# A layered attention and feed-forward kernel: its loops on every engine written out, with constants for registers

## What is computed

```python
x = L0_attn_x                                        # 4 x 1024 x 128
h = _layernorm(x) * (1 + ca) + sa
x = x + ga * softmax((h Wq + bq)(h Wk + bk)^T / sqrt(128)) (h Wv + bv)
h = _layernorm(x) * (1 + cb) + sb
for i in range(6):                                   # DEPTH
    q, k, v = split(shift_tokens(h) @ Wqkv[i], 3)    # 16 heads of 64
    q, k = rotary(l2norm(q) * qs), rotary(l2norm(k) * ks)
    h = local_attention(q, k, v, window=32) @ Wo[i] + h
    a, gate = split(norm(shift_tokens(h)) @ W1[i] + b1[i], 2)
    h = a * gelu(gate) @ W2[i] + b2[i] + h
x = x + gb * h
```

## Time and profile before

| | |
|---|---|
| median of 3 runs | 3659.52 us (3654.99 to 3666.93) |
| the profiled execution, its own time | 3657.72 us |
| its span, first to last instruction | 3655.9 us |
| mean granted TensorE clock | 0.970 |
| PE busy | 3440.4 us (94%) |
| PEld busy | 2655.9 us (73%) |
| DVE busy | 2639.6 us (72%) |
| ACT busy | 2510.0 us (69%) |
| POOL busy | 2356.1 us (64%) |

### The profile page before, as it was taken

One profiled execution on the slowest core, in us unless ns is written; L12 is line 12 of the kernel. 1 busy time (PEld: TensorE's weight loads), 2 busy tenths in 40 slices (PEclk: granted clock), 3 DMA queues, 4 the chain that ended last, 5 costly groups with the idle time before them and its releaser, 6 DMA issues.

```text
span 3655.9 us, 132252 instructions
## 1 busy us (share of the span) xinstructions
PE 3440.4 (94%) x50548; PEld 2655.9 (73%) x50548; DVE 2639.6 (72%) x5823; ACT 2510.0 (69%) x5117; POOL 2356.1 (64%) x1568
## 2 busy tenths in 40 slices
PE   7979999999999999999999999999999999999997
PEld 5658777777777777777777777777777777777774
DVE  5668777778777778777677777777767677777773
ACT  3447777777666777766677776677767677766773
POOL 2048677677666677666676766677766667666661
PEclk9989999999999999999999999999999999999998
DMA  2001111211111211111111111111111121111111
GB/s 80 2 14 49 34 44 41 62 41 50 36 42 37 62 37 51 40 35 43 58 41 37 50 41 35 50 54 38 52 35 39 36 65 40 47 40 39 41 37 44
DMA packets 98219, 157.34 MB, mean 43 GB/s; under 512 B 18128, under 2 KB 39632, under 8 KB 96720
## 3 DMA queue, kind: packets, MB, share of 16 engines
q1 hardware_dynamic: 93440, 132.73, 13.4%
q10 hardware_dynamic: 4176, 15.74, 1.3%
HBM read 20.48 MB, written 2.10 MB: 6 GB/s over the span
## 4 chain that ended last, share of the span: by engine, by line
PE 78%; issue 7%; ACT 5%; POOL 1%; DVE 1%; ACTq 0%; DMA 0%; DVEq 0%; POOLq 0%; SPq 0%
PE psum L797 20%; PE psum L821 12%; PE psum L887 9%; PE psum L907 7%; PE psum L844 6%; PE psum L864 4%; PE psum L852 4%; PE psum L927 4%; PE psum L939 3%; PE psum L932 3%; PE psum L816 2%; PE psum L918 1%; PE psum L914 1%; ACT probT L592 1%; ACT qbd L585 1%
## 5 line engine op out<-in xcount | busy, mean ns | idle before, releaser
L388 POOL TENSOR_TENSOR qkr<-qks,rnorm 128x1024 f32<-128x1024 f32 x384 | 731.3, 1905 | 388.0 <-issue 291.4
L380 POOL TENSOR_TENSOR qks<-work 128x1024 f32<-128x1024 f32 x384 | 908.0, 2365 | 72.2 <-DVE work L1148 67.9
L396 POOL TENSOR_TENSOR probn<-prob,psumr 128x512 f32<-128x512 f32 x384 | 400.6, 1043 | 542.9 <-DVE psumr L1174 542.9
L575 ACT ACTIVATE sq<-psum 128x512 f32<-128x512 f32 x768 | 463.9, 604 | 366.9 <-PE psum L797 366.2
L797 PE MATMUL psum<-whi,xhi 128*128 128x512 f32 x1152 | 571.8, 496 | 113.0 <-issue 79.1
L1122 DVE TENSOR_REDUCE ssq<-sq 128x8 f32<-128x512 f32 x768 | 516.6, 680 | 54.4 <-ACT sq L575 18.6
L1146 DVE TENSOR_TENSOR work<-psum,rot 128x512 f32<-128x512 f32 x768 | 508.3, 662 | 51.1 <-POOL qks L380 41.9
L1180 DVE TENSOR_REDUCE nmax<-psum 128x8 f32<-128x512 f32 x384 | 265.1, 690 | 380.7 <-PE psum L821 379.4
L821 PEld LDWEIGHTS psum<-kT,qbd 128*64 128x64 f32 x12288 | 411.6, 143 | 127.0 <-issue 126.8
L821 PE MATMUL psum<-kT,qbd 128*64 128x64 f32 x12288 | 468.5, 231 | 13.3 <-issue 13.2
L797 PE MATMUL psum<-whi,xlo 128*128 128x512 f32 x1152 | 464.5, 403 | 0.0
(11 more groups left out here) (131 smaller groups left out, 6488.8 us busy)
## 6 DMA issues: line engine op xcount, KB each, us to landing
vsh<-vtok SPq DMA_DIRECT2D x384, 192.0 KB, 2.4
vsh<-vtok SPq DMA_DIRECT2D x384, 64.0 KB, 3.0
xsh<-xs_in SPq DMA_DIRECT2D x192, 64.0 KB, 2.4
ff_x<-x_mid SPq DMA_DIRECT2D x96, 128.0 KB
wqkv<-Wqkv_dram ACTq DMA_DIRECT2D x5, 1536.0 KB, 6.7
wo_next<-Wo_dram ACTq DMA_DIRECT2D x5, 512.0 KB, 8.2
xtok<-x_dram SPq DMA_DIRECT2D x4, 512.0 KB, 11.0
out_dram<-qkr SPq DMA_DIRECT2D x8, 256.0 KB, 2.5
```

The source lines that it names most:

```text
L380: pool.tensor_tensor(qks[:, :, :], rcos, rsin, ALU.add).then_inc(s["add_ready"], 1)
L388: pool.tensor_tensor(qkr[:, j % 2, :, :], qks[:, :, :], rnorm[:, :].unsqueeze(2).to_broadcast([P, 2 * OCT, DH]), ALU.mult).then_inc(s["qkr ...
L396: pool.tensor_tensor(probn[:, :, :], prob[:, j % 2, :, :], psumr[:, j % 2, 1, :].unsqueeze(2).to_broadcast([P, OCT, KEYS]), ALU.mult).then ...
L575: act.activation(sq[:, w * OCT:(w + 1) * OCT, :], bank[w].rearrange("p (h n) -> p h n", n=DH), ACT.Square).then_inc(s[("sqq_ready", "sqk_r ...
```

## The change

Every engine's program is written out in Python over `STEPS + 2 * UNROLL` = 400 steps, with the absolute unit number n in place of a turn and its offset. There is no loop left on any engine, the output loops included, so every wait value, column and table entry is a constant. `Turn`, `sweep` and `wait_apart` are gone; `need` waits for a constant and is left out where that is zero or less; `block_at` and `renewed_at` say in which steps a feed-forward block or a weight renewal has its place. The same operations stand in the same order on each engine, with the same buffers. Five waits are new on PE: `ffn_mean`, `ffn_variance`, `ffn_up` and `ffn_down` also wait for `pts_ready`, and `output` always waits for `x_mid_ready`.

```diff
-        def need(eng, what, base, off, first=False):
-            if first and off <= 0:
-                return
-            eng.wait_ge(s[what], base + off)
-
-        def wait_apart(eng, *waits):
-            for k, (what, value) in enumerate(waits):
-                eng.reg_mov(counts_of[eng.engine][k], value)
-            eng.wait_ge(s["id_ready"], 1)
-            for k, (what, value) in enumerate(waits):
-                eng.wait_ge(s[what] if isinstance(what, str) else what, counts_of[eng.engine][k])
-
-
-
-        def sweep(eng, body):
-            def turn(layer, it, **more):
-                def v(e):
-                    return e if isinstance(e, int) else eng.snap(e)
-                early = isinstance(it, int) and it < 2
-                body(Turn(units=v(layer * UNITS + it * UNROLL), tiles=v(layer * TILES + it * TPI), block=v(layer * BLOCKS + it - 2),
-                          it=it, layer=v(layer), kb=(it - 2) % BLOCKS if isinstance(it, int) else v(it - 2),
-                          ffn_layer=v(layer - 1 if early else layer), **more))
-
-            turn(0, 0, first=True, ffn=False)
-            turn(0, 1, ffn=False)
-            with eng.Fori(2, ITERS - 1) as it:
-                turn(0, it)
-            with eng.Fori(0, DEPTH - 1) as layer:
-                turn(layer, ITERS - 1, renew=True)
-                turn(layer + 1, 0, renew=True)
-                turn(layer + 1, 1, renew=True)
-                with eng.Fori(2, ITERS - 1) as it:
-                    turn(layer + 1, it)
-            turn(DEPTH - 1, ITERS - 1)
-            turn(DEPTH, 0, last=True)
-            turn(DEPTH, 1, last=True, drained=True)
+        def need(eng, what, value):
+            if value > 0:
+                eng.wait_ge(s[what], value)
...
-                    def attend(j, u):
-                        if j is None:
-                            return
-                        tp, oc = j // UPT % 2, j % UPT
-                        wait_apart(pe, (vsh_in[j % 4], units * 8 + (j // 4 + 1) * 32), ("pts_ready", units + (j + 1)),
-                                   *([] if first and j <= 0 else [("aot_ready", units + j)]),
...
-                    def ffn_mean():
-                        pe.wait_ge(s["f_x"], t.block * 32 + 32)
-                        pe.wait_ge(s["f_out"], t.block)
-                        pe.matmul(bank[4], mean_mat[:, :], ff_x[:, :], start=True, stop=True).then_inc(s["f_m"], 1)
-
...
-                sweep(pe, body)
...
+            def attend(n, ffn_in_67):
+                if not is_unit(n):
+                    return
+                tp, oc = n // UPT % 2, n % UPT
+                pe.wait_ge(vsh_in[n % 4], (n // 4 + 1) * 32)
+                need(pe, "pts_ready", n + 1)
+                need(pe, "aot_ready", n)
+                if ffn_in_67 is not None:
+                    pe.wait_ge(s["f_u"], ffn_in_67 * CH + CH)
...
+            def output(n):
+                if not is_unit(n) or n % UPT == 0:
+                    return
+                tp, tile = n // UPT % 2, n // UPT
+                need(pe, "aot_ready", n + 1)
+                need(pe, "vs_ready", min(n + 4, STEPS))
+                need(pe, "x_mid_ready", tile)
...
+            def ffn_mean(b):
+                if b is None:
+                    return
+                pe.wait_ge(s["f_x"], b * 32 + 32)
+                need(pe, "f_out", b)
+                need(pe, "pts_ready", min(b * UNROLL + 2 * UNROLL - 5 + 1, STEPS))
+                pe.matmul(bank[4], mean_mat[:, :], ff_x[:, :], start=True, stop=True).then_inc(s["f_m"], 1)
...
+            for step in range(STEPS + 2 * UNROLL):
+                ffn_up(block_at(step, 4))
+                projection(step, 0)
+                ffn_down(block_at(step, 5))
+                scores(step - 3)
+                turn_q(step - 2)
+                turn_probabilities(step - 5, (block_at(step, 1), "f_xc", lambda b: b + 1), (block_at(step, 3), "f_ln", lambda b: b + 1),
+                                   (block_at(step, 4), "f_u", lambda b: b * CH + 1), (block_at(step, 5), "f_out", lambda b: b + 1))
+                value_projection(step - 3)
+                projection(step, 1)
+                turn_k(step - 2)
+                attend(step - 5, block_at(step, 4))
+                output(step - 6)
+                ffn_mean(block_at(step, 0))
+                ffn_variance(block_at(step, 2))
...
-                    def ffn_out():
-                        dve.wait_ge(s["f_y"], t.block + 1)
-                        dve.scalar_tensor_tensor(out=xs_in[:, bass.ds(t.kb * BLK + t.kb // 2 + HIST, BLK)], in0=bank[4],
-                                                 scalar=b2_col[:, bass.ds(t.ffn_layer, 1)],
-                                                 in1=x_mid[:, bass.ds(t.kb * BLK + t.kb // 2 + 1, BLK)], op0=ALU.add, op1=ALU.add).then_inc(s["f_out"], 1)
...
+            def ffn_out(b):
+                if b is None:
+                    return
+                layer, kb = b // BLOCKS, b % BLOCKS
+                dve.wait_ge(s["f_y"], b + 1)
+                col = kb * BLK + kb // 2 + 1
+                dve.scalar_tensor_tensor(out=xs_in[:, col:col + BLK], in0=bank[4], scalar=b2_col[:, layer:layer + 1],
+                                         in1=x_mid[:, col:col + BLK], op0=ALU.add, op1=ALU.add).then_inc(s["f_out"], 1)
```

More of the change, by code:

```diff
@@ L10 @@
 from contextlib import ExitStack
-from dataclasses import dataclass
 import concourse.bass as bass
@@ L57, with block_at, renewed_at, is_unit @@
 NORM_AT = {bw: n for n, bw in enumerate(NORMS)}
[L60 to L79, removed]
+def block_at(step, place):
+    b = step // UNROLL - 2
+    return b if step % UNROLL == place and 0 <= b < DEPTH * BLOCKS else None
+def renewed_at(step, place):
+    layer = (step - place) // UNITS
+    return layer if (step - place) % UNITS == 0 and 0 < layer < DEPTH else None
+def is_unit(n):
+    return 0 <= n < STEPS
 def build(nc, x, w_attn, b_qk, b_v, Wqkv, Wo, W1, W2, cols, b1_cols, gains, c_t, wmod, rot_tab, out):
@@ L245, in _ @@
             sp.dma_start(w2[:, :, :].rearrange("p k n -> p (k n)"), W2[0]).then_inc(s["w2_in"], 16)
[L247 to L260, removed]
-                sp.dma_start(dst[0:64], src[0:64, bass.ds(col, width)]).then_inc(signal, 16)
-                sp.dma_start(dst[64:P], src[64:P, bass.ds(col - 1, width)]).then_inc(signal, 16)
@@ L303, in _ @@
+            for step in range(STEPS + 2 * UNROLL):
+                x_half(step)
+                ffn_fetched(block_at(step, 0))
+                values_shifted(step - 4)
             out_v = out.rearrange("b (k t p) d -> (b k) p t d", t=4, p=P)
-            with sp.Fori(0, BLOCKS // 2) as i:
+            for i in range(BLOCKS // 2):
                 for h in range(2):
@@ L312, in _ @@
         def _(pool):
-            counts_of[pool.engine] = [pool.alloc_register(f"pool_count{k}") for k in range(2)]
             pool.memset(ident[:, :], 0.0).then_inc(s["id_zero"], 1)
@@ L451, in _ @@
         @block.scalar
         def _(act):
-            counts_of[act.engine] = [act.alloc_register(f"act_count{k}") for k in range(2)]
             act.preload_act_table_set("natural_log_exp_and_others")
@@ L693, in _ @@
         @block.tensor
         def _(pe):
-            counts_of[pe.engine] = [pe.alloc_register(f"pe_count{k}") for k in range(4)]
             pe.wait_ge(s["silu_ready"], 1)
@@ L962, in _, with project @@
-            pe.wait_ge(s["mask_ready"], 10)
-            attention()
-            with pe.Fori(0, BLOCKS // 2) as i:
+            def project(out, n, w):
+                ti, oc = n // UPT % TPI, n % UPT
+                if n % UNITS < UPT:
+                    pe.wait_ge(s["w_lo"], n // UNITS * len(SECTIONS) + ((0, 1), (2, 3), (4, 5))[oc if w < 2 else 2][w if w < 2 else oc] + 1)
+                for k, (xp, wp_) in enumerate(PARTS):
+                    mm = pe.matmul(out, xparts[xp][:, ti, :], wparts[wp_][:, w, oc * 512:(oc + 1) * 512], start=(k == 0), stop=(k == 2))
+                return mm
@@ new lines, in turn_probabilities @@
+            def turn_probabilities(n, *ffn_in_4):
+                if not is_unit(n):
+                    return
+                need(pe, "pn_ready", n + 1)
+                need(pe, "pts_ready", n)
+                for b, what, value in ffn_in_4:
+                    if b is not None:
+                        pe.wait_ge(s[what], value(b))
+                for a in range(PAIRS):
+                    mm = pe.transpose(bank[4][:, a * P:(a + 1) * P], probn[:, 2 * a:2 * a + 2, :].rearrange("p h n -> p (h n)"), ident[:, :])
+                mm.then_inc(s["pt_ready"], 1)
@@ new lines, in ffn_down @@
+            def ffn_down(b):
+                if b is None:
+                    return
+                pe.wait_ge(s["w2_in"], b // BLOCKS * 16 + 16)
+                pe.wait_ge(s["f_u"], b * CH + CH)
+                need(pe, "pts_ready", min((b + 2) * UNROLL, STEPS))
+                for ch in range(CH):
```

(18 more changed lines are left out.)

890 lines of the change are left out of this document (407 added, 483 removed).

## The result

The changed kernel takes 3473.51 us (median of 4 runs, 3472.59 to 3477.69), the kernel before 3662.82 us on the same chip (4 runs). The ratio is 0.9488, with a 95% interval of 0.9468 to 0.9507: 5.1% faster. The profiled execution took 3472.62 us, against 3657.72 us: 185.1 us less.

The account below looks back on a forecast made before the run. PE, busy 94% of the time, was taken as the bound. Jumps (175.4 us) and renewals (1.5 us), 176.9 us in all, off the profiled 3657.7 gave 3480.8, stated as 3480 us, range 3464 to 3502.

Parts of the forecast that it names:

- The jumps: PE's 28 loop turns with a jump back: 175.4 us would go, 6.3 us a jump.
- the same turn without a jump takes 66.0: Basis of the jump term: all 28 jumping turns, 72.3 us each, would take 66.0 us like an already written-out turn.
- Registers: Register work: DVE's ahead of the feed-forward result lies inside the 6.3 us a jump; nothing added, 8.4 us kept for the range.
- New waits: 384 added waits on PE, in feed-forward functions and output, already met earlier: zero in the sum, 19.6 us if none is hidden.
- Renewals: Weight renewals in the written-out turns: 1.5 us gained, as every layer should look like the 203.1 us three.
- the 7.5 us kept for it in the range: Allowance for each of five renewals meeting a half clock again, 1.5 us each.
- Fetching: Fetching the written-out program once in full: zero in the sum, one 1.10 us PE packet needed every 6.9 us.
- The rival of a late stream: PE would wait for its instruction packets in the 28 turns, 296 us, giving 3776 us, slower than before; chance 4%.
- Output and drain: Small output loop at the end loses three jumps and some register columns: nothing counted.
- The sum: Jumps plus renewals, 175.4 + 1.5 = 176.9 us, off the profiled 3657.7 us gives 3480.8 us.
- The next wait moves up: Rival: without jumps PE waits for lagging POOL, DVE or ACT; half of 6.3 us returns, 3568 us; chance 8%.
- The signs: Trace marks of being right: no PE branches, ordinary turns at 66.0 us, clock near 1.00, fewer than 480 PE fetch packets.

Follow-up runs that it names:

- experiment 2: Changed kernel with only PE back on loops and registers, the other four engines written out: 3661.36 us, 0.9993 of the kernel before.
- experiment 3: Kernel before with PE's inner loops written out, its outer loop (4 jumps) and most registers kept, other engines written out: 3508.30 us, 0.9575.
- experiment 5: Changed kernel plus a two-pass loop around one already met wait at the head of each of PE's 50 turns: 3473.09 us, 0.9477.
- experiment 6: Changed kernel plus four-pass loops of met waits, various sizes, behind the work on PE and ACT; only the jumps' times were read, no kernel time given.
- experiment 1: Changed kernel with only PE written out; SP, POOL, ACT and DVE keep the loops and registers of the kernel before: 3499.97 us, 0.955.
- experiment 9: Changed kernel without the 192 new waits for pts_ready in PE's four feed-forward functions: 3474.06 us, 0.9484.
- experiment 10: Changed kernel with ACT's exponential moved behind the attention copy in the steps with an up projection: 3463.47 us, 0.9455.
- experiment 4: PE with its outer loop alone, other engines written out, and ACT issuing the next layer's weights two steps later: 3494.15 us, 0.9536.

## Why the prediction was right

- **The jumps, 175.4 us.** Right, 176.7 measured. The step "the same turn without a jump takes 66.0" held to 0.05 us a turn, or 1.3 us in all. Experiments 2 and 3 show that PE's jumps carry some 170 us of it, and 5 and 6 that distance decides. The other 6.4 us are step 5 with DVE's registers, as the prediction says when it puts them inside the 6.3 us a jump. Its 6.3 us was a mean over unlike jumps (2.9 and 6.9), which the sum didn't need to know.
- **What the prediction did not see** is that the other engines' outer jumps are worth 24 us once PE's are gone (experiment 1). It read the earlier trace rows as if ACT's 45 ns meant that ACT jumps free. For the inner loop that is true. For the outer one the record is as short, and the stall lies behind it. The number came out right because the change takes away both; for a change of PE alone it would have been 26.5 us too low. The sum took these stalls in, since it compares with turns in which no engine jumps; the mechanism told with it left them out. The rows of before held the hint: of the ten waits for `xlo` in the earlier trace rows, 27.9 us, I gave five to the renewals at the group's mean of 2.8 us. Read one by one, the renewals' five take 2.1 each, one of 2.8 stands ahead of the turns, and the other four, 14.5 us, 3.2 to 3.9 each, stand at the outer jumps, where POOL and ACT came late themselves.
- **Registers: zero beyond the turn of the earlier trace rows.** Right. In experiment 3 PE's cost nothing, in 1 DVE's cost 0.1 us a turn at most. Both together, in before, cost 0.23 us in each loop turn, which the comparison with the turn of the earlier trace rows already took in.
- **New waits: zero, bound 19.6 us.** Right, by experiment 9 for half of them. For the 192 in `output` no run takes them out; the 65.95 us, below the 66.0 of the turn without them, speak for zero.
- **Renewals: 1.5 us.** 3.1 measured: the first trio gave 1.8, the others 0.3 each. The half clock at a renewal comes and goes: in experiment 10 three of five renewal turns take 70.4 to 70.5 us and two 68.9. So some of the 7.5 us kept for it in the range can occur.
- **Fetching: zero.** Right. 404 packets over the span, 65.95 us in every ordinary turn, and no idle time of PE over 0.4 us in one. The threes of before had fetched 25 packets each and not the 29 of the rival's text, and after needs one every 8.0 us. The rival of a late stream fell, and with it the doubt that bursts of 9 ns an instruction could drain the buffer. The rows say why: 404 packets for 101096 matmuls and weight loads are some 250 a packet, which at 9 ns last 2.3 us, and a packet takes 1.1 us, so even a burst is no faster than its fetches (an estimate).
- **Output and drain: "I count nothing".** The drain gave 4.6 us, the largest error. From the last feed-forward result to the end, before took 3655.9 - 3635.7 = 20.2 us and after 3470.6 - 3452.2 = 18.4 us: the 1.8 us between fit the output loops that the term left out, though no run takes these out alone. The other 2.8 us came ahead of it. One output projection of before's drain took 3.61 us in the chain, at 3597.4 us, where the clock record falls to 0.5 for 3.4 us; after's takes 1.98. The drain of before has 31.3 us at half clock, that of after 23.2. So part of this gain is where the half clock fell, and that I can't forecast.
- **The sum.** 1.3 (turns) + 0.4 (turns 6 and 46) + 0.5 (ramp) + 1.6 (renewals) + 4.6 (drain) = 8.4 us more than 176.9 left the span, all in the same direction, so the profiled execution took 3472.6 and not 3480.8 us.
- **The next wait moves up.** It did not: L863 waits 8.2 us for ACT, as L927 did.
- **The signs.** All that were named for "right" came, but one: the waits of L797 and L821 were to be under 15 us, and 16.0 are left, 3.5 of them ahead of the layers.

## What to carry to other kernels

On the engine that bounds the kernel, count the instructions of a loop's body: below the step (here between 1536 and 1792 on PE, between 320 and 384 on ACT) a jump back takes 0.1 to 0.4 us, beyond it 3.3 us and more on PE and 2.3 us and more on ACT, plus the half clock that followed most of PE's far jumps here. A stall of the bounding engine hides those of the others at the same place, so write out a loop on all engines or expect the next one's jump to surface. If a far jump has to stay, keep large transfers away from it.

## What I had not expected

- PE's branch record holds the stall (3.3 to 7.6 us); on ACT, DVE and POOL the branch reads 40 to 67 ns and the stall is idle time behind it, as "issue". A short branch record is no proof of a cheap jump.
- A far jump of PE takes 6.0 to 7.4 us when 2 MB of weights are under way and 3.6 to 3.9 us when they are not (experiments 3 and 4). The inner jumps of before take 3.3 to 3.8 us in layer 0 and 4.3 to 5.4 us later, with no weights under way in either; why they differ is open.
- The loops of four engines, with 5600 instructions more (132252 against 126655), are all but invisible in the time of the kernel before: experiment 2, without them, is as slow within its interval. There ACT's weights, sent on time, meet PE's fetch: the branches of its outer jumps take 7.3 to 7.6 us.
